# First norm and residual batch by batch in two fused operations, and the router's exponentials between two groups of scalings, in a one-core transformer layer

## The reference

```python
x = x + attn(cond(x, ...), wq, wkv, wo, gamma, beta)      # windowed attention, then its layer norm
#   y = ...;  out = (y - mean) * rsqrt(var + eps) * gamma + beta
x = x + ffn(cond2(x, ...), W1, b1, W2, b2, Wr, br)
#   cond2: ctx = causal_ema(x);  wg = sigmoid([x, ctx] @ Wg.T + bg);  gated = x * wg
#          mod = 0.5 + sigmoid(gelu(x @ Wn1.T + bn1) @ Wn2.T + bn2)      # 8 factors a token
#          temporal = sum over d of softmax(blend)[d] * causal_ema_d(gated * mod[d])
#          gate = sigmoid(temporal @ Wtemp.T + btemp);  soma = gelu(x @ Wsoma.T + bsoma)
#          z = layernorm((soma * gate) @ Wout.T) * gamma + beta
#   ffn:   logits = z @ Wr + br;  expert = argmax;  gate = softmax(logits) at the expert
#          y = gelu(z @ W1[expert] + b1) @ W2[expert] + b2, times the gate
```

## Time and profile before

| | |
|---|---|
| median of 3 runs | 210.94 us (209.81 to 213.72) |
| time of the profiled execution | 211.43 us |
| its span | 209.6 us, mean granted TensorE clock 0.873 |
| busy: PE / DVE / ACT / POOL | 170.8 / 119.0 / 115.5 / 71.6 us |
| share of PE in the chain that ended last | 49% (DVE 11%, POOL 6%, ACT 6%) |

### The profile page before, as it was taken

How to read it: one execution, slowest core, us unless ns; L and a number is a source line. 1 busy time by engine, 2 the same in 40 slices (tenths; PEclk the granted TensorE clock), 3 DMA queues, 4 the chain that set the end, 5 groups by cost and what they waited for, 6 DMA issues and landing times.

```text
span 209.6 us, 4787 instructions
## 1 busy us (share of the span) xinstructions
PE 170.8 (81%) x1666; PEld 129.1 (62%) x1666; DVE 119.0 (57%) x360; ACT 115.5 (55%) x270; POOL 71.6 (34%) x109
## 2 busy tenths in 40 slices
PE   1959868999999886999989949999861169999970
PEld 1426747677766453466658636999751059999960
DVE  6475685646786555252262589598456525665620
ACT  2668823668766976688764815511476015655530
POOL 8999830200530005000020010000240277777761
PEclk9979955589999997599999966999995559999998
DMA  4455435417653254352000699400003034224200
GB/s 125 114 150 128 116 107 177 129 13 181 153 99 34 82 178 86 57 184 84 3 0 3 170 360 290 84 0 3 3 0 98 5 104 109 78 61 67 60 9 0
DMA packets 22191, 19.41 MB, mean 93 GB/s; under 512 B 4398, under 2 KB 19490, under 8 KB 22168
## 3 DMA queue, kind: packets, MB, share of 16 engines
q1 hardware_dynamic: 20376, 16.44, 29.7%
q0 software_dynamic: 1232, 2.51, 5.2%
q10 hardware_dynamic: 560, 0.16, 0.3%
HBM read 8.40 MB, written 2.04 MB: 50 GB/s over the span
## 4 chain that ended last, share of the span: by engine, by line
PE 49%; SPq 14%; DVE 11%; issue 7%; POOL 6%; ACT 6%; DMA 4%; DVEq 0%; ACTq 0%; POOLq 0%
SPq L410 7%; PE ps L935 6%; PE ps L892 5%; PE ps L1068 5%; PE ps L872 4%; PE ps L650 4%; PE ps L645 4%; POOL out_dram L631 4%; PE ps L1081 4%; PE ps L861 4%; PE ps L753 3%; PE ps L739 2%; PE ps L716 2%; DMA t_cols<-in_L_cond_b_self_dram 2%; ACT t_rows L1357 1%
## 5 line engine op out<-in xcount | busy, mean ns | idle before, releaser
L1374 ACT ACTIVATE t_v_pad<-ps,t_b_tile 128x128 f32<-128x128 f32 x60 | 17.2, 369 | 24.2 <-PE ps L1068 24.2
L1462 DVE TENSOR_REDUCE t_mx<-ps 128x4 f32<-128x512 f32 x32 | 21.7, 687 | 12.2 <-PE ps L716 11.7
L603 POOL TENSOR_SCALAR t_rstd<-t_mv 128x4 f32<-128x4 f32 (+2 forms) x5 | 1.4, 273 | 65.5 <-DVE t_mv L1535 65.5
L1219 ACT ACTIVATE t_P<-ps 128x512 f32<-128x512 f32 x32 | 19.0, 598 | 7.0 <-PE ps L861 6.1
L1193 ACT ACTIVATE t_P<-ps 128x512 f32<-128x512 f32 x32 | 18.9, 602 | 6.0 <-ACT t_negmT L1199 3.2
L620 POOL DMA_INDIRECT t_Qs<-z_dram,t_perm x15 | 14.8, 986 | 15.1 <-DVE t_perm L1726 10.8
L1068 PE MATMUL ps<-t_zsT,t_late 128*128 128x128 f32 x120 | 17.4, 293 | 0.0
L1595 DVE SCALAR_TENSOR_TENSOR t_Qs<-t_v_pad,t_mod,t_blend 128x128 f32<-128x128 f32 x64 | 17.1, 346 | 0.1
L631 POOL DMA_INDIRECT out_dram<-t_v_pad,t_perm x15 | 15.3, 1019 | 5.3 <-issue 4.7
L1081 PE MATMUL ps<-t_Ks,t_v_pad 128*128 x120 | 16.7, 282 | 0.0
L1068 PEld LDWEIGHTS ps<-t_zsT,t_late 128*128 128x128 f32 x120 | 16.1, 209 | 0.2 <-DVE t_zsT L1742 0.2
(11 more groups left out here) (290 smaller groups left out, 356.1 us busy)
## 6 DMA issues: line engine op xcount, KB each, us to landing
t_Qs<-t_parts SPq DMA_DIRECT2D x24, 128.0 KB
t_Ks<-t_parts SPq DMA_DIRECT2D x24, 128.0 KB
t_Ks<-in_L_ffn_W_dram SPq DMA_DIRECT2D x1, 2048.0 KB, 9.7
t_Ks<-t_key_residue SPq DMA_DIRECT2D x8, 128.0 KB, 2.4
t_Qs<-t_query_residue SPq DMA_DIRECT2D x8, 128.0 KB, 2.5
z_dram<-t_rows SPq DMA_DIRECT2D x2, 258.0 KB, 3.6
t_rows<-in_fside_BxSxS_dram SPq DMA_DIRECT2D x2, 256.0 KB, 3.2
t_x_tok<-in_x_dram SPq DMA_DIRECT2D x2, 256.0 KB, 3.7
```

The lines of the kernel that those rows point to most:

```text
L1219: act.activation(P[:, (UNITS + u) % 3, :], ps[u % 4][:, :], ACT.Sigmoid, scale=SCALE).then_inc(window_scores_read, 1)
L1462: dve.tensor_reduce(mx[:, b, 4 * g:4 * g + 4], MAX_BANKS[u % 2][:, :].rearrange("p (j t) -> p j t", j=4), AX.X, ALU.max).then_inc(max_scor ...
```

## The change

The first norm runs by batch. `inverse_std` on POOL is called once per batch with one column. On DVE `norm_half` is gone, and `add_norm(b, step)` has two fused operations on one batch of 128 by 128: step 0 takes (x1 - mean) * gamma, right behind the statistics of the batch and without waiting for `rstd`; step 1 takes that times `rstd`, plus `xb`, two turns later, and signals `x1_ready` once per batch. For batch 7 step 1 stands after the loop, behind `modulate(0)`. Those who waited for half 1 or 2 of x1 now wait for 4 or 8 batches, and the counts of `rstd_ready` for the second norm move from 3 and 5 to 9 and 11. On ACT the exponentials go between `scale_z(0)` and `scale_z(1)`.

```diff
-            inverse_std(0, range(0, HALF))
-            inverse_std(0, range(HALF, NB))
+            for b in range(NB):
+                inverse_std(0, range(b, b + 1))
...
-                pe.wait_ge(x1_ready, half + 1)
+                pe.wait_ge(x1_ready, HALF * (half + 1))
                 transposes(f"x1T_{half}", lambda i: x1[:, half * HALF + i, :], 4)
...
             scale_z(0)
-            scale_z(1)
             act.wait_ge(lgm_sub, 1)
             act.activation(gexp[:], gexp[:], ACT.Exp).then_inc(gexp_ready, 1)
+            scale_z(1)
...
-            def norm_half(n, buf, half, gamma, into, addend, done):
-                bs = slice(half * HALF, half * HALF + HALF)
-                dve.wait_ge(rstd_ready, n + 1)
-                for b in range(half * HALF, half * HALF + HALF):
-                    m = dve.tensor_scalar(buf[:, b, :], buf[:, b, :], mv[:, b, 0:1], rstd[:, b:b + 1],
-                                          ALU.subtract, ALU.mult)
-                link(m)
-                link(dve.tensor_tensor(buf[:, bs, :], buf[:, bs, :], bc_mid(gamma[:], HALF), ALU.mult))
-                link(dve.tensor_tensor(into[:, bs, :], buf[:, bs, :], addend, ALU.add), done)
...
-            def add_norm(half):
-
-                if half == 0:
+            def add_norm(b, step):
+
+                if b == 0 and step == 0:
                     dve.wait_ge(ld_g1, 32)
                     dve.wait_ge(xb_ready, 1)
-                norm_half(half, x1, half, gamma1, x1, xb[:, half * HALF:half * HALF + HALF, :], x1_ready)
-
+                if step == 0:
+                    dve.wait_ge(mv_ready, b + 1)
+                    dve.scalar_tensor_tensor(x1[:, b, :], x1[:, b, :], mv[:, b, 0:1], gamma1[:], ALU.subtract, ALU.mult)\
+                        .then_inc(x1_scaled, 1)
+                if step == 1:
+                    dve.wait_ge(x1_scaled, b + 1)
+                    dve.wait_ge(rstd_ready, b + 1)
+                    dve.scalar_tensor_tensor(x1[:, b, :], x1[:, b, :], rstd[:, b:b + 1], xb[:, b, :], ALU.mult, ALU.add)\
+                        .then_inc(x1_ready, 1)
...
                     residual(u // G)
-                    if u // G == HALF - 1:
-                        add_norm(0)
+                    add_norm(u // G, 0)
+                u = t - WINDOW_AT - LAG_WOUT - 3
+                if 0 <= u < UNITS and u % G == G - 1:
+                    add_norm(u // G, 1)
...
             mod_sums(0)
             modulate(0)
-            add_norm(1)
+            add_norm(NB - 1, 1)
+            dve.wait_ge(x1_ready, NB)
```

More of the change, by code:

```diff
@@ L338, in fused_layer @@
         mv_ready, rstd_ready = sem("mv_ready"), sem("rstd_ready")
-        x1_ready, xb_ready = sem("x1_ready"), sem("xb_ready")
+        x1_ready, x1_scaled, xb_ready = sem("x1_ready"), sem("x1_scaled"), sem("xb_ready")
         band_ready, residue_in = sem("band_ready"), [sem(f"residue_in{i}") for i in range(2)]
@@ L477, in _ @@
                 bs = slice(half * HALF, half * HALF + HALF)
-                sp.wait_ge(x1_ready, half + 1)
+                sp.wait_ge(x1_ready, HALF * (half + 1))
                 sp.dma_start(token_rows[:, bs, 0:D], x1[:, bs, :]).then_inc(x1_out, 16)
@@ L1580, in gated_inputs @@
                 dve.wait_ge(gate_sig, half + 1)
+                dve.wait_ge(x1_ready, HALF * (half + 1))
                 dve.tensor_tensor(wgate[:, bs, :], wgate[:, bs, :], x1[:, bs, :], ALU.mult).then_inc(gated_ready, 1)
@@ L1678, in _ @@
                 bs = slice(half * HALF, half * HALF + HALF)
-                dve.wait_ge(rstd_ready, (3, 5)[half])
+                dve.wait_ge(rstd_ready, (NB + 1, NB + 3)[half])
                 dve.scalar_tensor_tensor(zshift[:, bs], mv[:, bs, 0], -1.0, rstd[:, bs], ALU.mult, ALU.mult)\
```

## The result

The changed kernel takes 203.3 us in the median of four executions (202.44, 202.92, 203.68, 205.63), against 210.81 for the kernel before in the same session: a ratio of 0.965 (0.959 to 0.971). The profiled execution is the longest of the four: 205.63 us, span 203.9, mean granted clock 0.895.

A forecast was written before the change was run, and what follows sets the result against it. PE's pause between window attention and traces, the half clock behind it and cond2's tail were taken as the bound. The sum was 211.43 - 2.5 - 2.3 - 1.05 = 205.6 us, range 204.3 to 208.2.

The forecast's parts named there:

- What bounds the kernel: PE's 4.1 us wait between window attention and traces, with the clock falling to half in its pause, plus cond2's tail.
- Term A: Second half's x1: PE starts its transposes at 121.55 instead of 124.04, gaining 2.5 us; bounds 2.0 and 2.7.
- the first half's gain: PE some 0.4 ahead after the first half's x1, eaten at the copy to `pv_sb`, leaving `y_7` and the aggregate unmoved.
- the 0.4 given as the bound: Sign of being right: PE idle under 0.4 us ahead of the second half's first transpose.
- Term B: Second half up to the traces: clock stays at 1.00 once the pause is gone, 2.3 us; bounds 0 and 2.5.
- the clock falls anyway: Rival, chance 0.20: the second half still runs at half clock, Term B falls away, 207.9 us.
- the wait for the products of batch 4: Sign of being wrong: PE waiting in the traces for DVE's products at batch 4, where the cover was 0.6 us.
- Term C: Tail of cond2: exponentials after four scalings of z, ranking behind PE's bank, permutation 1.05 us earlier; bounds 0.45 and 1.15.
- the rival on the landing: Chance 0.08: the landing of z's writes comes last, behind the permutation, so Term C is 0.45 and the time 206.2.
- The half-rate rule: Fused steps with two non-bf16 SBUF sources run at half throughput; rival at chance 0.03, 0.7 us more, 206.3.
- The slower case: Rival, chance 0.05: POOL's pair above 1.4 us in the window part delays the residuals; at 2.4 the kernel takes 212.4.
- How the numbers follow: Chances of the cases and the range 204.3 to 208.2: low end 205.1 by better bounds, less 0.8 for scatter of executions.

The follow-up runs named there:

- e_warm: The kernel before with five matmuls, results used nowhere, in PE's pause before the second half's transposes, and a wait keeping their bank free: 207.42 us, ratio 0.986.
- r_after3: The changed kernel once more, unaltered, in a third session: 205.09 us, ratio 0.971 against the kernel before.
- r_after: The changed kernel run again, unaltered, in the session after the first: 205.93 us, ratio 0.974 against the kernel before.

## Why the prediction was right or wrong

**What bounds the kernel.** Right: PE's pause between window and traces was on the path, and its length and the clock behind it were the price.

**Term A, 2.5.** Right in its sum. From `y_3` to the second half's transposes the change takes 2.65 off. The 1.6 from aggregate to transposes came as forecast; step 1 took 0.35, the pair on POOL 1.02 (1.11 was forecast) with its first operation at 0.37 beside step 0 (0.44 was assumed). One part was mis-sized: the first half's gain was to be 0.4, all of it eaten at the copy to `pv_sb`. By PE's rows `y_3` to the first half's transposes fell by 0.62 (5.81 to 5.19), and from there to `y_7` 0.36 came back (9.55 to 9.91). So `y_7` kept 0.26, which the prediction names as a sign of being wrong, and the aggregate of batch 7 kept 0.16, since step 1 of batch 6 stands ahead of `residual(7)`. The idle time of PE, 0.54, is over the 0.4 given as the bound: counted from `y_3`, PE ended soma of the first half 0.48 earlier than before, where the forecast had it at nearly the same time.

**Term B, 2.3.** Right: 2.38 in the table, and `e_warm` shows its cause by itself. The rival that the clock falls anyway in the second half did not come in any profile of the changed kernel, nor the wait for the products of batch 4 (the 80 trace instructions take 8.93 as before).

**Term C, 1.05.** Right in the profiles, 1.02 from the ranking to the permutation; in the time it is not shown. In the first profile z's writes were the last to land by a little, as the rival on the landing had it: POOL waited for them, which the prediction names as a sign of being wrong, and the first tile came 0.16 later behind the permutation. In the other three profiles the permutation was last (`r_after3`, the view of waits):

```profile
POOL t_Qs L620 <- DVE t_perm L1727: 10.4, 1, 10.4
```

What the forecast had not seen is that the term shrinks to 0.3 or 0.4 where the clock falls ahead of the logits. Its lower bound, 0.45, was worked out for another cause.

**The half-rate rule.** Step 0 and step 1 took 0.35 each, as long as the L1541 of before (0.346 in the mean of its eight), which have that shape and one tensor source, so here too the trace does not bear out the rule of the Trainium skill that the prediction names.

**The slower case.** Its condition did not come near: the pair took 0.90 to 1.02 where 1.4 was the threshold, and DVE waits for `y_b` for 9.3 us in seven turns, where it was 13.6.

**The step that failed** is the range in "How the numbers follow", and the anchor that it shares with the sum. The sum started from one profiled execution and gave a later median only 0.8 us of room below, half of the distance from that execution to the lowest of three. Yet the three shown were already 3.9 apart, and a median of three or four of them can stand off by more than 0.8. The runs show the size: executions of the changed kernel spread over 4.9 us, and the medians of the four sessions are 203.3, 205.9, 206.2 and 205.1. Of the 2.3 us between 205.6 and 203.3, 0.6 is the anchor (211.43, against a median of 210.81 of the kernel before in that session), and 1.7 is gain beyond the sum: 7.5 in that session against 5.85, where the other three gave 4.6, 4.8 and 6.1. The mechanism's sum, 5.85, stands beside 6.05 by landmarks in the profiles. That the forecast, 205.6, stands so near 205.3 over all executions is partly luck: the anchor is 0.7 above the median of all executions of the kernel before, 210.75, and the difference of the medians, 5.5, is 0.35 below the sum, and the two errors work against each other. With a room of 2 us, about half of the spread of the three, the low end would have been 203.1; that is said with the result known.

**What stays open.** Why three of the first four executions lay at 202.4 to 203.7, where 4 of the 18 later ones lie below 204. If that share holds for all, three or more in four come about 4 times in 100; a difference between chips is not excluded, and the intervals of the four ratios overlap. The clocks on record (0.902 to 0.911 for these three) speak for fewer falls of the clock and against a gain without a name, but no profile of an execution of the changed kernel under 203.8 was taken, so that is not shown.

## What to carry to other kernels

Price a stall together with the clock that it costs: here the pause was 2.7 us and the half clock behind it another 2.4, and five matmuls whose results nobody reads bought the second without touching the first. Before a range is drawn around a sum from one profile, look at how far the executions shown lie apart, and give the median room by it; half of it on each side would have been enough here. And when work ahead of a transfer gets quicker, look for the next place where the program waits for that transfer: here part of the gain was given back there.

## What the runs showed of the hardware

POOL's one-column addition took 0.37 to 0.38 us in seven of its eight turns, where it began 0.05 behind DVE's step 0, and 0.24 in the first turn, where it began 0.06 ahead of it; in the second norm, with no such operation beside it, it took 0.21 to 0.22. DVE's step 0 kept its 0.35 in each. The first turn of the changed kernel:

```profile
94.10 0.24 POOL L603 TENSOR_SCALAR t_rstd<-t_mv 128x1 f32<-128x1 f32 x1 [11.64 <-DVE t_mv L1535]
94.16 0.35 DVE L1553 SCALAR_TENSOR_TENSOR t_rows<-t_rows,t_mv,t_gamma 128x128 f32<-128x128 f32 x1
```

The table load on ACT (1.28) is followed by the exponentials 0.02 later (151.49 + 1.28 to 152.79). Whether the clock falls differs between executions of one program at the same place: at the window's start it stayed at 1.00 behind waits of 0.74 and 1.00 us in `r_after`, and in `r_after3`, with waits of 0.25 and 1.49, it fell to 0.50 within the second. And a wait for a transfer can stand in the profile as "issue": the stand ahead of batch 4 got its releaser only when the copies were spread over two queues.
